# A four-layer decoder: one-head attention in staggered rounds, chosen rows for one expert layer, and smaller moves of order

## Chip, cores and metric

The kernel runs on one core of a Trainium2 chip. The metric is the device time of one execution in microseconds (us).

## What is computed

x is [8 batches, 256 tokens, 128 features] in float32, ctx has the same shape, and the mask is [8, 1, 256, 256]. Four layers follow one another. Each adds three terms to x, each computed from a layernorm of x as it then stands:

```python
x = x + L0_attn(ln(x));  x = x + L0_xattn(ln(x), ctx);  x = x + L0_ffn(ln(x))
x = x + L1_attn(ln(x));  x = x + L1_xattn(ln(x), ctx);  x = x + L1_ffn(ln(x))
x = x + L2_attn(ln(x));  x = x + L2_xattn(ln(x), ctx);  x = x + L2_ffn(ln(x))
x = x + L3_attn(ln(x));  x = x + L3_xattn(ln(x), ctx, mask);  x = x + L3_ffn(ln(x))
```

L0_attn, L0_xattn and L2_attn are softmax attention with 16 heads of 8 features, with fixed masks. L1_attn is stick-breaking attention with 16 heads. L3_xattn has 16 heads and adds the mask that is passed in. Three attentions have one head of 128 features. L1_xattn multiplies the scores by 1 + sigmoid(gate), where the gate is a second product of tanh projections. L2_xattn is causal, with projections. L3_attn has q = k = v = ln(x), and a token sees only those whose distance is a multiple of 4. L1_ffn has 8 experts of 512 hidden columns, and each expert chooses its own tokens:

```python
probs = softmax(x @ gate_w.T)                    # 256 tokens x 8 experts, per batch
g, m = top_k(probs.transpose(0, 2, 1), k=64)     # each expert takes its 64 best tokens
h = gelu(x[m] @ w1[e]) @ w2[e]
out[m] += g * h
```

L2_ffn has 16 experts (two per token, with a capacity), L3_ffn has 8 experts and a shared one.

## The kernel before

The whole of x stays in SBUF as `x_resid`, 16 tiles of 128 tokens by 128 features, two tiles per batch. The decoder (L2458) is a row of **stages**. Each is one or two blocks, in which every engine has its own instruction list, and between two blocks all engines wait for each other. A stage's name stands ahead of its buffers' names. The order is load, L0a, L0x (`quad_heads`, L435), L0n (`normalize_and_turn`, L2032), L0f (`experts`, L2163), L1a (`stick_heads`, L1340), L1x (`single_head`, L1748), L1n, L1r (`route_expert_choice`, L2292), L1f, the transfers of `load_last_experts` (L406), L2a (`quad_heads`), L2x (`single_head`), L2n, L2r, L2f, L3a (`single_head`), L3x (`masked_heads`, L936), L3n, L3r, L3s, L3f, store. The engines are PE (matmul), DVE (vector), ACT (activations, copies), POOL and SP (issues DMAs).

**`layernorm_scales`** (L117) is a block of its own ahead of each stage: ACT loads a table, then computes ln and exp of all 16 tiles' variances to get rstd. The stage's own block starts with another table load.

**`quad_heads`** treats the heads four at a time, side by side in row groups of 32. A batch has 6 slots. A slot is two score banks (`score`, L584; `hide_score`, L592, adds a fixed mask with a bf16 matmul), of which DVE takes the maxima (L864), and two banks of logits (L600) from the same products, from which the negated maximum is subtracted (`shift`), which are masked (`hide`), go through exp on ACT and are weighed with v (L645). Scores run one slot ahead of the logits. Since batch 0 has nothing to run behind, its slots come first, alone, in only two PSUM banks: DVE must reduce a bank before PE may refill it. **`masked_heads`** is alike with 8 slots. Its maxima include the mask that is loaded (L1277, four of 128x256 per slot), and PE adds the mask to the logits as three bf16 parts (L1107). Scores are one slot ahead. At the end of a batch the maxima are gathered, turned on PE (`turn_max`, L1129), negated (L1292) and only then may the next batch's logits be shifted (L1098).

**`single_head`** runs its 8 batches in a hardware loop, and the buffers (`h`, `hT`, `e`, `eT`, `y`) exist once. PE's order for a batch is scores (and gate scores L1859), turn the next h, turn exp(scores), project the next batch, weigh (L1885), and for L1x turn y (L1895), output projection. DVE takes the maximum, divides (L2005) or adds (L2013), and takes the new mean and variance of x. POOL copies the batch's ctxT into `cT`, DVE its v. In L3a the next h is made only after weighing, since h is also v.

**`normalize_and_turn`** normalizes two tiles, turns them on PE, copies them on ACT and multiplies with the router's weights, pair after pair. **`route_expert_choice`** takes the 64 best tokens of each of 64 (batch, expert) rows by eight rounds of max-8 on DVE. It leaves `gates`, zero for a token not chosen. **`experts`** for L1f runs all 2048 tokens through each of the 8 experts, batch by batch in a hardware loop. For a batch and expert PE issues 4 up matmuls of 256 columns (L2225) and 8 down matmuls of 128 columns (L2211), all recorded in halves. ACT computes two Gelu of 128x512 (L2246), DVE multiplies with the gate and adds to x (L2264).

**`load_last_experts`** is a block in which SP alone works. It issues 8 DMAs, 7.7 MB, with the weights of L2f and L3f. They may not be issued earlier, since their buffers overlap with those of earlier weights.

## Time and profile before

| what | us |
|---|---|
| device time, median of 3 runs | 2542.66 (2542.03 to 2544.7) |
| device time of the profiled execution | 2542.87 |
| its span | 2541.1 |
| PE busy in the span | 2014.9 (79%) |
| DVE busy | 1020.4 (40%) |
| ACT busy | 833.4 (33%) |
| POOL busy | 374.1 (15%) |

A stage is found in the timeline by the names of its buffers. For a stretch, the profile gives each engine's busy time, the number of instructions and PEclk, the granted share of TensorE's full clock (0.50 is 1.2 GHz, 1.00 is 2.4 GHz). The same instruction has a longer duration at the lower clock. A row of the timeline can hold several like instructions, merged, and a matmul can be recorded in two halves.

### The profile page before, as it was taken

Reading aid. Unit: us, or ns where it says so; the run is one execution under the profiler, and the core shown is the slowest. Engines: PE = TensorE matmul, PEld = TensorE weight load, DVE = VectorE, ACT = ScalarE, POOL = GpSimd, SP = SyncE. Lnnn points to the kernel's source line nnn. Section 1 sums busy time; section 2 is a strip of 40 time slices with the busy share of each in tenths; the row PEclk is TensorE's granted clock in tenths of the full one; section 3 lists DMA queues with packets and bytes.
Section 4 is the critical chain, followed back from the end, with each engine's and each line's share of the span. In section 5 each row is a group of like instructions: output and inputs, shape, how many; then the busy total and the mean of one; then the engine's idle time right before and its main releaser. Section 6 shows DMA issues by size and latency. Waiting matters only on the chain. (4 is left out here: it accounts for less than half of the span.)

```text
span 2541.1 us, 39338 instructions
## 1 busy us (share of the span) xinstructions
PE 2014.9 (79%) x13413; PEld 1346.0 (53%) x13413; DVE 1020.4 (40%) x2899; ACT 833.4 (33%) x1606; POOL 374.1 (15%) x458
## 2 busy tenths in 40 slices
PE   3898688669999564899759975499975599984998
PEld 2344244354444343799724444399953255553887
DVE  3454355334555232222125623333333355523444
ACT  2244144315777222233203432233321133332221
POOL 4331433002110000000034400000000533300000
PEclk8799599887999665899959988599975598995999
DMA  4000000000000000000120000000000000000000
GB/s 138 1 2 1 1 1 1 1 0 1 1 1 1 0 0 0 1 0 0 46 76 2 1 1 0 1 0 0 0 0 0 13 9 10 6 1 0 0 0 17
DMA packets 20029, 21.15 MB, mean 8 GB/s; under 512 B 2660, under 2 KB 15176, under 8 KB 19912
## 3 DMA queue, kind: packets, MB, share of 16 engines
q1 hardware_dynamic: 19912, 19.59, 2.4%
q8 instruction: 73, 1.20, 0.2%
q14 instruction: 44, 0.36, 0.0%
HBM read 18.54 MB, written 1.05 MB: 8 GB/s over the span
## 5 line engine op out<-in xcount | busy, mean ns | idle before, releaser
L1277 DVE CUSTOM_DVE_ANT_0 L3x_junk<-L3x_psS,L3x_mask_rows 128x256 f32<-128x256 f32 x256 | 98.6, 422 | 124.6 <-PE L3x_psS L1081 106.5
L1240 ACT ACTIVATE scores_L_experts_L<-L3x_psL 128x512 f32<-128x512 f32 x128 | 76.4, 597 | 199.4 <-PE L3x_psL L1107 196.1
L2211 PEld LDWEIGHTS L2f_psY<-scores_L_experts_L,L2f_hidden 128*128 128x128 f32 x1024 | 134.1, 193 | 8.9 <-issue 2.6
L2225 PE MATMUL L2f_psG<-hT,scores_L_experts_L 128*128 x512 | 132.5, 384 | 6.5 <-DVEq L86 6.5
L2211 PE MATMUL L2f_psY<-scores_L_experts_L,L2f_hidden 128*128 128x128 f32 x1024 | 136.0, 277 | 0.0
L2264 DVE SCALAR_TENSOR_TENSOR x_resid<-L2f_psY,L2f_gate,x_resid 128x128 f32 x256 | 78.1, 347 | 133.5 <-PE L2f_psY L2211 131.4
L2246 ACT ACTIVATE L2f_hidden<-L2f_psG 128x512 f32<-128x512 f32 x128 | 76.4, 597 | 152.4 <-PE L2f_psG L2225 152.4
L2246 ACT ACTIVATE L1f_hidden<-L1f_psG 128x512 f32<-128x512 f32 x128 | 76.4, 597 | 148.8 <-PE L1f_psG L2225 148.8
L2225 PE MATMUL L1f_psG<-hT,experts_L_L 128*128 x512 | 123.4, 385 | 2.2 <-ACTq L43 2.2
L2211 PEld LDWEIGHTS L1f_psY<-experts_L_L,L1f_hidden 128*128 128x128 f32 x1024 | 123.1, 192 | 2.9
L2211 PE MATMUL L1f_psY<-experts_L_L,L1f_hidden 128*128 128x128 f32 x1024 | 123.4, 275 | 0.0
L2264 DVE SCALAR_TENSOR_TENSOR x_resid<-L1f_psY,L1f_gate,x_resid 128x128 f32 x128 | 39.0, 347 | 170.9 <-PE L1f_psY L2211 170.9
L1107 PE MATMUL L3x_psL<-identb,L3x_mask_parts 128*128 128x256 bf16 x768 | 103.5, 289 | 0.0
L2225 PEld LDWEIGHTS L1f_psG<-hT,experts_L_L 128*128 128x128 f32 x512 | 93.5, 193 | 15.7 <-issue 5.3
L2225 PEld LDWEIGHTS L2f_psG<-hT,scores_L_experts_L 128*128 128x128 f32 x512 | 89.4, 194 | 14.6 <-issue 7.2
L1081 PE MATMUL L3x_psS<-L3x_km,L3x_qT 32*128 32x512 f32 x256 | 84.2, 738 | 13.6 <-DVE L3x_mx L1277 13.2
L2246 ACT ACTIVATE L3f_activated<-L3f_psG 128x512 f32<-128x512 f32 x72 | 43.0, 597 | 152.7 <-PE L3f_psU L2225 152.7
L804 ACT ACTIVATE L0x_probs<-L0x_psL 128x512 f32<-128x512 f32 x96 | 52.1, 595 | 121.2 <-PE L0x_psL L628 86.7
L2279 DVE TENSOR_TENSOR L3f_hidden<-L3f_activated,L3f_psU 128x512 f32<-128x512 f32 x72 | 49.5, 688 | 103.1 <-ACT L3f_activated L2246 103.1
L1089 PE MATMUL L3x_psL<-L3x_qm,ctx_T 32*128 32x512 f32 x256 | 75.7, 666 | 17.4 <-DVE L3x_mx L1277 17.0
L804 ACT ACTIVATE L2a_probs<-L2a_psL 128x512 f32<-128x512 f32 x96 | 52.1, 595 | 114.1 <-PE L2a_psL L626 84.3
L1107 PEld LDWEIGHTS L3x_psL<-identb,L3x_mask_parts 128*128 128x128 bf16 x768 | 73.5, 103 | 25.5 <-issue 14.7
(657 smaller groups left out, 4321.4 us busy)
## 6 DMA issues: line engine op xcount, KB each, us to landing
...
```

The lines of the kernel that those rows point to most:

```text
L804: nc.scalar.activation(probs[:, half, a, k, :], psL[i % RING][:], ACT.Exp, scale=scale).then_inc(s_prob, 1)
L1081: nc.tensor.matmul(psS[a][:], qT[rows, b % 3, t * P:(t + 1) * P], km[rows, b % 2, 2 * pair:2 * pair + 2, :], start=True, stop=True).then_i ...
L1089: nc.tensor.matmul(bank[:], mem.ctxT[rows, b * S + u * P:b * S + (u + 1) * P], qm[rows, b % 3, 2 * pair:2 * pair + 2, :], start=True, stop ...
L1107: last = nc.tensor.matmul(at[:, :, t * P:(t + 1) * P], parts[:, b % 2, i, t, u * P:(u + 1) * P], two, start=False, stop=i == PARTS - 1, sk ...
L1240: nc.scalar.activation(probs[:, half, a, k, :], psL[i % RING][:], ACT.Exp).then_inc(s_prob, 1)
L1277: last = nc.vector.tensor_tensor_reduce(out=junk[:, i, :], in0=psS[a][:, i * S:(i + 1) * S], in1=mrow[:, b % 2, t, :], scale=1.0, scalar=L ...
L2211: last = nc.tensor.matmul(psY[j % 2][:, t * D:(t + 1) * D], hid[:, j % 2, c, t * P:(t + 1) * P], members[j][3][:, c, :], start=c == 0, sto ...
L2225: last = nc.tensor.matmul(bank[u % 2][:, i * S:(i + 1) * S], weight[:, c * P:(c + 1) * P], source[:, bass.ds(b * S, S)], start=True, stop= ...
L2246: nc.scalar.activation(dst, psG[u % 2][:, 0:n * S].rearrange("p (c s) -> p c s", c=n), func).then_inc(s_act.sem, 1)
L2264: last = nc.vector.scalar_tensor_tensor(at, psY[j % 2][:, t * D:(t + 1) * D].unsqueeze(1), gate[:, t, members[j][4]:members[j][4] + 1], at ...
L2279: nc.vector.tensor_tensor(hid[:, j % 2, g[0]:g[0] + n, :], act_out[:, u % 2, 0:n, :], psU[u % 2][:, 0:n * S].rearrange("p (c s) -> p c s", ...
```

## The change

- The ln and exp of `layernorm_scales` move into the ACT list of the stage's own block, for all attention stages and for L1n, L2n, L3n.
- `quad_heads` (L0a, L0x, L2a): batch 0's scores come in 3 rounds of four banks (`first_scores`) in place of 6 slots of two, and later slots issue `hide_score` directly behind `score`, ahead of `shift` and `hide`.
- `load_last_experts` goes. SP issues the same 8 DMAs inside L2a's block.
- `masked_heads` (L3x): 4 opening rounds of four banks; scores run two slots ahead of the logits; the maxima and their negation have two buffers each; gathering, turning and negating the maxima come earlier, ahead of the last slots' shift.
- `lone_head` replaces `single_head`: no hardware loop, rounds in which the engines work on batches i+2 to i-2, two to four buffers of each tile, ctx and ctxT read in place. For L1x the gate's 0.5 and 1.5 are folded into one instruction and POOL adds the output bias to x. L3a's mask is one matmul of 256 columns in place of two of 128.
- `turn_and_route` replaces `normalize_and_turn` for L1n, L2n, L3n: four chunks of four tiles, each chunk with a PSUM bank of its own.
- `choose_by_expert` replaces `route_expert_choice`: besides choosing, it gives each chosen token its rank (1 to 64), by six small f32 matmuls. `chosen_experts` replaces `experts` for L1f. It makes 0/1 matrices from the ranks (DVE, two of 128x512 per batch), gathers the chosen 64 rows per expert and batch with two matmuls of 512 columns per batch, and runs 512 rows per expert instead of 2048: 32 steps of one up matmul of 512 columns, a Gelu and `widen`, and 16 down matmuls of 128 columns per expert. `widen` spreads a pair of batches' ranks and gates over 64 rows each with four matmuls of 256 columns, ACT copies the gates and DVE makes the scatter matrix (`keep_put`). Last, `scatter` adds up, per pair of batches, 8 experts in 32 matmuls of 64 rows by 128 columns.

```diff
+def last_experts(w, dram):
...
-    with nc.Block() as block:
-        @block.sync
-        def _(sp):
-            for dst, src in loads:
-                sp.dma_start(dst, src).then_inc(w["late"], 16)
-    w["late_count"] += 16 * len(loads)
...
-        layernorm_scales(nc, mem, name, scales)
...
+        w["late_count"] += 16 * len(loads)
         with nc.Block() as block:
+            if loads:
+                @block.sync
+                def _(sp):
+                    for dst, src in loads:
+                        sp.dma_start(dst, src).then_inc(w["late"], 16)
...
+                def first_scores(k):
+                    if k == 0:
+                        pe.wait_ge(s_km, 1)
+                    else:
+                        pe.wait_ge(s_red, 4 * k)
+                    t, u = KINDS[k]
+                    hidden = mask.scores[k]
+                    for r in range(4):
+                        rows = slice(32 * r, 32 * r + 32)
+                        last = nc.tensor.matmul(first_banks[r][:], qT[rows, 0, t * P:(t + 1) * P], km[rows, 0, :, u * P:(u + 1) * P],
...
+                    if b == 1:
+                        first_scores(0)
...
-                for m in range(SLOTS + 1):
-                    free_score_banks(m)
-                    for a in range(2):
-                        score(m, a)
-                    for a in range(2):
-                        hide_score(m, a)
-                    if m == SLOTS - 1:
-                        turn_max(0)
+                for k in range(1, 3):
+                    first_scores(k)
+                free_score_banks(SLOTS)
+                for a in range(2):
+                    score(SLOTS, a)
+                for a in range(2):
+                    hide_score(SLOTS, a)
+                turn_max(0)
                 for b in range(B):
...
+                            for a in range(2):
+                                hide_score(m, a)
...
-                        if ahead:
-                            for a in range(2):
-                                hide_score(m, a)
...
+                nc.scalar.activation(mem.lnv[:], mem.mv[:, :, 1], ACT.Ln, bias=mem.eps[:]).then_inc(scales, 1)
+                act.wait_ge(scales, 1)
+                nc.scalar.activation(mem.rstd[:], mem.lnv[:], ACT.Exp, scale=-0.5).then_inc(scales, 1)
...
-    SCORE_AT = ((0, 0), (2, 0), (2, 1), (2, 2), (2, 3), (0, 1), (0, 2), (0, 3))
+    SCORE_AT = ((0, 0), (0, 1), (2, 0), (2, 1), (2, 2), (2, 3), (0, 2), (0, 3))
...
+                for k in range(4):
+                    first_scores(k)
+                turn_max(0)
...
-                        m = SLOTS * (b + 1) + n + 1
+                        m = SLOTS * (b + 1) + n + 2
...
+                        if n == 6 and b > 0:
+                            project(b - 1)
+                        if n == 7 and b + 1 < B:
+                            turn_max(b + 1)
...
-                        if n == 6 and b > 0:
-                            project(b - 1)
-                        if n == 7 and b + 1 < B:
-                            turn_max(b + 1)
...
-                        if n == 7:
-                            if b + 1 < B:
-                                negate(b + 1)
...
-def single_head(nc, mem, w, name, kind):
...
+def lone_head(nc, mem, w, name, kind):
...
+    HB, TB = 4, 3
...
+                            last = nc.tensor.matmul(bank[:, t * S:(t + 1) * S], mem.identb[:], w["same"][:].unsqueeze(1).to_broadcast([P, TPB, P]),
...
+                for i in range(B + 2):
+                    if i < B:
+                        score(i)
+                    if gnosis and 0 <= i - 2:
+                        turn_y(i - 2)
+                    if not dilated and i + 1 < B:
+                        project(i + 1)
+                    if 0 <= i - 1 < B:
+                        turn_exp(i - 1)
+                    if gnosis and 0 <= i - 2:
+                        finish(i - 2)
+                    if i + 2 < B:
+                        turn(i + 2)
+                    if 0 <= i - 1 < B:
+                        weigh(i - 1)
 
...
+                for i in range(B + 2):
+                    if gnosis and i < B:
+                        gate(i)
+                    if gnosis and 0 <= i - 2:
+                        keep_y(i - 2)
+                    if not dilated and i + 1 < B:
+                        keep_projections(i + 1)
+                    if 0 <= i - 1 < B:
+                        keep_exp(i - 1)
+                    if i + 2 < B:
+                        keep_h(i + 2)
+                    if i < B:
+                        exponent(i)
...
+                        nc.vector.scalar_tensor_tensor(mixed[:, b % 2, :, :], sig[:, b % 2, :, :], 3.0,
+                                                       psS[b % 2][:].rearrange("p (t k) -> p t k", t=TPB), ALU.add, ALU.mult).then_inc(s_mixed, 1)
...
+                for i in range(B + 2):
+                    if i + 2 < B:
+                        normal(i + 2)
+                    if i < B:
+                        maximum(i)
+                    if causal and i + 1 < B:
+                        keep_v(i + 1)
+                    if 0 <= i - 1 < B:
+                        invert(i - 1)
+                    if gnosis:
+                        if 0 <= i - 2:
+                            add(i - 2)
+                        if 0 <= i - 1 < B:
+                            divide(i - 1)
+                        if 0 <= i - 2:
+                            stats(i - 2)
+                    elif 0 <= i - 1 < B:
+                        add(i - 1)
+                        stats(i - 1)
...
+def turn_and_route(nc, mem, w, name, gate, n, logits, hT=None, h_all=None):
...
+                turn(0)
+                for c in range(CHUNKS):
+                    if c + 1 < CHUNKS:
+                        turn(c + 1)
+                    pe.wait_ge(s_hT, c + 1)
+                    for t in range(c * CHUNK, (c + 1) * CHUNK):
+                        last = nc.tensor.matmul(psR[:, t * n:(t + 1) * n], hT[:, t * P:(t + 1) * P], gate, start=True, stop=True)
+                    last.then_inc(s_routed, 1)
...
+def choose_by_expert(nc, mem, w, name, logits, place, place_rows, gate_rows, E, keep):
...
+                pe.wait_ge(s_marked, 1)
+                nc.tensor.matmul(psK[:, 0:R], w["earlier"][:], marked[:, 0, :], start=True, stop=True)
+                nc.tensor.matmul(psK[:, R:2 * R], w["ones"][:], marked[:, 0, :], start=True, stop=False)
+                nc.tensor.matmul(psK[:, R:2 * R], w["earlier"][:], marked[:, 1, :], start=False, stop=True)
+                nc.tensor.matmul(psK[0:R, S:S + P], marked[:, 0, :], w["earlier"][:], start=True, stop=True)
+                nc.tensor.matmul(psK[0:R, S + P:2 * S], marked[:, 0, :], w["ones"][:], start=True, stop=False)
+                nc.tensor.matmul(psK[0:R, S + P:2 * S], marked[:, 1, :], w["earlier"][:], start=False, stop=True).then_inc(s_ranked, 1)
...
+def chosen_experts(nc, mem, w, name, h_all, place, place_rows, gate_rows, w1, w2, spread_at, E, keep):
...
+                def keep_put(i):
+                    c, e = divmod(i, E)
+                    dve.wait_ge(s_gate, i + 1)
+                    nc.vector.scalar_tensor_tensor(put[:, c, e, :], psB[i % 2][:, 0:S], w["slot_col"][:, 0:1], wide[:, i % 2, :],
+                                                   ALU.is_equal, ALU.mult).then_inc(s_put, 1)
...
+                def widen(i):
+                    c, e = divmod(i, E)
+                    if i >= 2:
+                        pe.wait_ge(s_put, i - 1)
+                    r = 2 * c * E + e
+                    for part, rows_of, one in ((0, place_rows, mem.identb), (1, gate_rows, mem.ident)):
+                        for k in range(2):
+                            last = nc.tensor.matmul(psB[i % 2][keep * k:keep * k + keep, part * S:part * S + S],
+                                                    one[0:R, r + E * k:r + E * k + 1].to_broadcast([R, keep]), rows_of[:],
+                                                    start=True, stop=True, skip_group_check=True)
+                    last.then_inc(s_wide, 1)
...
+                def scatter(c):
+                    pe.wait_ge(s_put, (c + 1) * E)
+                    if c >= 1:
+                        pe.wait_ge(s_x, 2 * c)
+                    for t in range(TPB):
+                        for e in range(E):
+                            for i in range(2):
+                                rows = slice(keep * i, keep * i + keep)
+                                last = nc.tensor.matmul(psX[i][:, t * P:(t + 1) * P], put[rows, c, e, t * P:(t + 1) * P],
+                                                        inner[rows, e, c * P:(c + 1) * P], start=e == 0, stop=e == E - 1)
+                                if t == TPB - 1 and e == E - 1:
+                                    last.then_inc(s_out, 1)
...
+                for e in range(E):
+                    for c in range(CHUNKS):
+                        up(e, c)
+                        widen(e * CHUNKS + c)
+                    if e > 0:
+                        down(e - 1)
+                down(E - 1)
+                pe.wait_ge(s_y, E)
+                for c in range(PAIRS):
+                    scatter(c)
+
...
+        lone_head(nc, mem, w, "L1x", "gnosis")
...
+            turn_and_route(nc, mem, w, "L1n", w["L1_ffn_gate_w"][:], 8, logits, h_all=h_all)
+            choose_by_expert(nc, mem, w, "L1r", logits, place, place_rows, gate_rows, 8, keep)
+            chosen_experts(nc, mem, w, "L1f", h_all, place, place_rows, gate_rows, w["L1_ffn_w1"], w["L1_ffn_w2"],
+                           w["scores"][:, 0:(B // 2) * 8 * S], 8, keep)
...
+                   wk_rot=w["L2_attn_Wk_rot"][:], wv=w["L2_attn_Wv"][:], wo=w["L2_attn_Wo"][:], mask=causal, scale=qk, loads=last_experts(w, dram))
...
```

## Rows read from the trace of the kernel before

**Rows 1.** Windows, one for each changed stage, columns as headed
```profile
core 0: us, PE busy (x) PEld busy (x) DVE busy (x) ACT busy (x) POOL busy (x), PEclk, DMA share, GB/s
42.00:256.00 214.00, 178.41 (x1496) 86.69 (x1496) 96.44 (x208) 79.13 (x150) 66.73 (x77) 0.87 0.00 1
838.50:985.50 147.00, 92.00 (x288) 58.47 (x288) 42.70 (x128) 34.82 (x85) 3.35 (x8) 0.59 0.00 0
985.50:1014.50 29.00, 10.85 (x48) 9.96 (x48) 8.20 (x24) 7.97 (x19) 0.00 (x0) 0.50 0.00 0
1028.00:1261.00 233.00, 228.60 (x1536) 212.25 (x1536) 49.41 (x176) 77.70 (x129) 0.00 (x0) 0.99 0.00 0
1261.00:1281.00 20.00, 0.00 (x0) 0.00 (x0) 0.00 (x0) 0.11 (x1) 0.00 (x0) 0.50 0.98 349
1504.00:1594.90 90.90, 46.86 (x200) 36.66 (x200) 31.13 (x112) 22.82 (x77) 3.27 (x8) 0.76 0.00 0
1875.20:1974.00 98.80, 50.98 (x176) 35.16 (x176) 30.13 (x112) 18.91 (x52) 0.00 (x0) 0.50 0.00 0
1974.00:2287.00 313.00, 264.22 (x2166) 142.77 (x2166) 143.98 (x616) 96.86 (x166) 103.84 (x116) 0.86 0.03 8
```

**Rows 2.** Timeline of L2a's opening (start us, duration, work [idle before, releaser])
```profile
1280.89 1.28 ACT L122 ACT_TABLE_LOAD   x1 [26.13 <-PEq L418]
1283.01 2.66 POOL L492 MEMSET L2a_v<- 128x3072 f32 x1 [331.95 <-SPq L489]
```

**Rows 3.** Timeline of L0a's score opening, and its PE waits (total, times, longest)
```profile
61.24 2.08 PE L584 MATMUL L0a_psS<-L0a_km,L0a_qT 32*128 32x512 f32 x4
63.89 1.29 DVE L864 TENSOR_REDUCE L0a_mx<-L0a_psS 128x4 f32<-128x512 f32 x2 [1.50 <-PE L0a_psS L592]
...
84.11 0.18 DVE L868 TENSOR_TENSOR L0a_mx<-L0a_mx_part 128x16 f32<-128x16 f32 x1
...
PE L0a_psL L600 <- DVE L0a_mx L864: 9.7, 8, 1.5
```

**Rows 4.** Timeline of L1x, tanh, product and division of one batch
```profile
882.79 0.78 ACT L1930 ACTIVATE L1x_tanh<-L1x_psG,b_gate,w_gate 128x512 f32<-128x512 f32 x1 [5.10 <-PE L1x_psG L1859]
884.17 0.69 DVE L1985 SCALAR_TENSOR_TENSOR L1x_mixed<-L1x_psS,L1x_tanh 128x512 f32<-128x512 f32 x1
892.58 0.42 DVE L2005 TENSOR_TENSOR L1x_y<-L1x_psO,L1x_rec 128x256 f32<-128x256 f32 x1 [5.40 <-PE L1x_psO L1885]
```

**Rows 5.** Timeline of L3a, a batch's weighing and its addition to x
```profile
1898.65 2.05 PE L1885 MATMUL L3a_psO<-L3a_h,L3a_eT 128*128 128x128 f32 x8 [0.77 <-ACT L3a_eT L1952]
1901.94 0.60 DVE L2013 SCALAR_TENSOR_TENSOR x_resid<-L3a_psO,L3a_rec,x_resid 128x128 f32 x2
```

**Rows 6.** Timeline of L1r, turning the chosen rows back
```profile
1026.42 0.47 PE L2354 MATMUL L1r_psC<-ident,L1r_chosen 64*128 64x64 f32 x2 [8.77 <-DVE L1r_chosen L2335]
```

**Rows 7.** Timeline of L1f: down, up, Gelu; and of L2a's last weighing
```profile
1034.44 1.95 PE L2211 MATMUL L1f_psY<-experts_L_L,L1f_hidden 128*128 128x128 f32 x16
1036.23 1.89 PE L2225 MATMUL L1f_psG<-hT,experts_L_L 128*128 x8
1037.37 0.60 ACT L2246 ACTIVATE L1f_hidden<-L1f_psG 128x512 f32<-128x512 f32 x1 [2.13 <-PE L1f_psG L2225]
...
1487.86 0.64 PE L645 MATMUL L2a_psO<-L2a_probs,L2a_v 128*32 128x256 f32 x8
```

**Rows 8.** Timeline of L3x: an opening slot; logits, scores and shift between batches
```profile
1986.52 2.08 PE L1081 MATMUL L3x_psS<-L3x_km,L3x_qT 32*128 32x512 f32 x4 [1.91 <-DVE L3x_mx L1277]
2116.86 0.70 PE L1089 MATMUL L3x_psL<-L3x_qm,ctx_T 32*128 32x512 f32 x2 [1.98 <-DVE L3x_mx L1277]
2118.83 0.61 PE L1098 MATMUL L3x_psL<-L3x_neg_max,quad_sel 32*128 32x256 bf16 x4 [0.82 <-DVE L3x_neg_max L1292]
```

**Rows 9.** The page: queue of instruction fetches (packets, MB, share); L3x's maxima on DVE
```profile
q8 instruction: 73, 1.20, 0.2%
...
L1277 DVE CUSTOM_DVE_ANT_0 L3x_junk<-L3x_psS,L3x_mask_rows 128x256 f32<-128x256 f32 x256 | 98.6, 422 | 124.6 <-PE L3x_psS L1081 106.5
```

742 lines of the change are left out of this document (487 added, 255 removed).

## The prediction, made before the run

> **What bounds the kernel now.** I read the windows by stage first [rows 1]. No engine bounds the program as a whole; each stage has its own limit, and the reader should see three kinds. In L1f PE is busy 228.6 of 233 us at a granted clock of 0.99, so only less work on PE shortens it. In L0a and L3x PE is busy 178.4 of 214 and 264.2 of 313, so waits in the opening and between batches are what an order can save. In the one-head layers nothing is full: L1x has PE 92 of 147 us, DVE 43, ACT 35, at a clock of 0.59; L3a has PE 51 of 98.8 at 0.50 (1.2 GHz). There the chain of one batch sets the time, and PE, waiting in between, is not given its full clock. L1n has PE 10.9 of 29, and for 20 us ahead of L2a only the DMA works (0.98 busy).
>
> The sum is made against the profiled run, 2542.87 us, of which 1.8 lie outside the span. It is 0.2 above the median. About 0.2%, or 5 us, is what a measurement of this kernel can tell from no change.
>
> **Scales in the stage's block.** The separate block's table load starts 2.12 us before the stage's own, and the stage's POOL work starts with the latter [rows 2]. In L0a, L0x, L2a, L1a and L3x that much goes: -2.1 each. For the other stages it is inside their sums.
>
> **quad_heads (L0a, L0x, L2a).** In the opening a slot's two scores take 2.08, then DVE's two maxima 1.29, and PE waits for them; from the first score at 61.24 to the gathering of the maxima at 84.11 the six slots take 22.9, 3.8 each [rows 3]. With four banks, four scores lie in four row groups and I take the same 2.1 for them; DVE then has four maxima, 4 x 0.65 = 2.6, of which the first starts half a us after its mask. A round is 5.1 to 5.7, and part of the first lies beside values(1): three rounds cost 17.4, so -5.5. `hide_score` ahead of `shift` lets DVE start its maxima about a us sooner in each slot; PE's waits for them ahead of the logits are 9.7 us in all in L0a [rows 3]. Not all of a wait can go, since DVE stays the slower of the two in the slots next to a batch's end: I take -4 between 0 and -10. Together -11.6 a stage, -34.8 for three, and -2.1 for L1a.
>
> **lone_head.** With staggered batches a round costs what its fullest engine needs. PE's work at full clock is busy time times PEclk [rows 1]: L1x 92.0 x 0.59 / 8 = 6.8 a batch, L2x 46.9 x 0.76 / 8 = 4.5, L3a 51.0 x 0.50 / 8 = 3.2. DVE's work a batch is 5.3, 3.9 and 3.8, ACT's 4.4, 2.9 and 2.4.
> L1x today takes about 17 a batch (147 less some 10 at its ends, by 8), in which ACT waits 5.1 for the gate scores and DVE 5.4 for weighing [rows 4]. The bias matmuls and one DVE pass leave; so a round is PE's 6.4: 8 x 6.4 = 51, plus 8 to the first scores, 4 for rounds at the low clock, 8 for the two rounds that drain, 1.3 for the barrier: 73, against 147: -74. POOL now adds the bias, 8 short additions beside 6.4 us rounds, free unless PE's `finish` waited for them, which DVE's `add` alone does.
> L2x: 8 x 4.45 = 35.6, start 9.5 (h, turn, projections, scores, one after another), low clock 3, drain 6.5, barrier 1.3, 1 for waits: 57, against 90.9: -34.
> L3a keeps a chain across rounds on DVE: weighing, then adding to x (0.60 [rows 5]), stats, the next h in two passes of 128x256 (0.42 each, as the division [rows 4]), which PE turns before it weighs again. Weighing takes 2.05 at 1.2 GHz [rows 5], 1.0 at full clock, and the round comes to 4.3: 8 x 4.3 = 34.4, start 9, low clock 3, drain 5, barrier 1.3: 53, against 98.8: -46.
> What is late next in all three is PE itself; each round is priced at the full clock. L1x's rounds keep PE busy nearly without a gap, as L1f does today. L3a's are busy 3.2 of 4.3, the least sure.
>
> **turn_and_route.** PE's 10.9 us at 1.2 GHz [rows 1] stay; with four banks only the first chunk's normalization (with rstd, 2.5) and the last copy and barrier (1.2) lie outside it: 14.5 of 29, so -14.5 in L1n and L2n and -15 in L3n: -44. The full clock would take up to 5 more off each.
>
> **choose_by_expert.** Behind the choosing come six f32 matmuls of 64 to 128 columns at the low clock. Two transposes of 64 columns are 0.47 [rows 6], so six are about 2, then a copy and two short DVE steps, part of them beside PE: +3 (between +2 and +5).
>
> **chosen_experts (L1f).** At full clock 8 down matmuls of 128 columns go by in 1.79 from start to start, 4 up matmuls of 256 in about 1.75 [rows 7]; so 0.22 a down matmul and 0.87 for 512 columns. Now per stage: 2.0 to the first 0/1 matrices; gather 8 x 2 x 0.87 = 14, with waits for DVE's matrices (two of 128x512 a batch, 0.7 each as the product in [rows 4]) and the clock's start 17.5; 0.8 for the last copy; 32 up matmuls, and 32 `widen`, each of two f32 and two bf16 matmuls of 256 columns, 2 x 0.43 + 2 x 0.11 = 1.1 one after another, 0.55 if the two column halves lie side by side. The nearest row is L2a's weighing, four f32 matmuls of 256 columns in four column groups in 0.64 [rows 7], where one after another they would be 1.73: side by side plus 0.2. So 0.85 for `widen` with its entry, 1.05 for `up` with its own, 32 x 1.9 = 61. Down: 128 x 0.22 with a drain each time, 8 x 4.1 = 33. ACT has a Gelu (0.60) and a copy (0.4) per step, DVE 0.45: both within 1.9. Scatter: 32 matmuls of 0.22 are 7.0 one after another, half of it side by side; I take 5.6, plus 2.1 in which PE waits for DVE's addition: 4 x 7.7 = 31. With 1 ahead of it and 1.5 at the end: 148, against 233: -85. Bounds: 128 if nothing is paid for going from one shape to the other and halves run together, 171 if all halves run one after another and the scatter waits more.
> The Trainium skill, "TensorEngine Tiling (Array Packing)", Tiling Modes, Key Properties, says that tiles of one shape run in parallel and that changing the shape drains the array. That rule speaks against alternating `up` and `widen`. The trace agrees as far as the side-by-side weighing goes; what the drain costs no row shows alone, and by the rule two changes a step at the 0.2 above would be 13 of the 61, which is already in it.
>
> **Transfers in L2a.** The 20 us alone go [rows 1]. Their cover is L2a, 210 us long, which itself loads nothing; L2f needs them 300 us later. What they can delay is instruction fetch and SBUF access in L2a's opening: 0 to +20. I take 0: the transfers write buffers that no engine touches in L2a, and no row shows one stage slowed by another's DMA.
>
> **L3x.** -2.1 for the scales. The opening's eight slots of 4.0 (2.08 of scores behind a wait of 1.91 [rows 8]) become four rounds of 2.1 + 8 maxima of 0.422 [rows 9] + 0.3 = 5.75, 23 in all, and one slot more comes ahead of the loop: -4 to -5. Between batches PE waits 1.98 for the maxima ahead of the logits and 0.82 ahead of the shift [rows 8]; with scores two slots ahead and the maxima turned earlier most of these 2.8 go at 7 boundaries: -19. DVE gains no work (144 of 313 busy). -25, between -5 and -33.
>
> **Sum.** -34.8 - 2.1 - 74 - 44 + 3 - 85 - 20 - 34 - 46 - 25 = -362. 2542.9 - 362 = 2181.
>
> **The rivals.**
> (a) PE is not given its full clock in the one-head rounds. For it: all three are at 0.50 to 0.76 now, L3a at 0.50 throughout. Then a round is PE's work at 1.2 GHz: L1x 12.8 less what the first rounds had anyway, +37; L2x +25; L3a 6.4, +13: 2256. Chance 9%. In L3a alone: 2194, in the main case's range.
> (b) The halves of `widen` and scatter run one after another: +23, 2204. For it: no row shows f32 halves of 64 columns. Against it: four groups of 32 do run together. 17%.
> (c) The transfers, or fetching the longer unrolled code, hold up L2a's opening and the new stages: +20, 2201. 12%.
> (d) The ends of the stages are better than taken, L1f at 128 and L2n, L3n at a higher clock: 2150. 17%.
> (e) The hidden cover isn't there in L3x and quad_heads, DVE being the one that sets their slots: the 19 and 3 x 4 stay, 2212. 8%.
> (f) Slower: the instruction stream. Loops become straight code, so some 60 more fetches of 16 KB are needed than today's 73 [rows 9]. If each held all engines up by more than 362 / 60 = 6 us, the gain would be gone, 2550. Against it: 73 fetches leave PE 79% busy today, and L0a's straight code, 178 of 214 busy, shows no such holes. 1.5%.
> That the change does not do what it says, no overlap in the rounds because a wait ties batch i to i-1, would leave the one-head layers as they are: 2335, 2%.
>
> **How the numbers follow.** The main case has 33%, at 2181 with 2165 to 2197 as its own range. With (b), (c), (d), (e) and half of (a), 2130 to 2250 holds about 8 in 10. Faster by over 0.2% is every case but (f): 0.98; within 0.2% 0.005; slower 0.015.
>
> **What the profile after would show.** L1x, L2x and L3a in windows of about 73, 57 and 53 us with PEclk above 0.85; if it is near 0.5, (a). L1f of 148 with a step of 1.9 between Gelus; 2.5 means (b). Nothing between L1f's and L2a's barrier, and the queue q1 busy inside L2a; gaps on all engines there mean (c). No wait of 1.98 ahead of L3x's logits between batches. L1n, L2n and L3n of 14 to 15. The prediction is wrong if the rounds are set by chains between engines longer than PE's work, which adds 8 us per us of round in each one-head stage.

## The result, and the profile after

The changed kernel takes 2120.09 us (median of 4 runs, 2119.14 to 2122.51), the kernel before 2543.68 beside it: a ratio of 0.8336, with a 95% interval of 0.8322 to 0.8351. The forecast was 2181 with a range from 2130 to 2250. The direction and the places were right, but 61 us more went than forecast. The profiled run's span is 2120.8 us.

I measure a stage from the last named instruction of the stage ahead to its own last one, so that the barrier counts, and set it beside the sum's terms. L0a alone is taken from its first instruction to L0x's, since the loading ahead of it moves by 3 us from run to run. The barrier between L0a and L0x, 2.1 us shorter, so stands in both rows, and the column adds up to 424.5 where the two profiled spans differ by 420.3; the loading took 1.4 us more in the changed kernel's, and the rest is spread over stages that the change leaves alone.

| stage | before | after | measured | forecast |
|---|---|---|---|---|
| L0a | 214.0 | 206.0 | -7.9 | -11.6 |
| L0x | 231.5 | 217.8 | -13.8 | -11.6 |
| L1a | 277.0 | 274.4 | -2.6 | -2.1 |
| L1x | 146.0 | 58.9 | -87.1 | -74 |
| L1n, L2n, L3n together | 96.5 | 46.6 | -49.9 | -44 |
| L1r | 13.0 | 16.8 | +3.7 | +3 |
| L1f | 231.1 | 124.2 | -106.8 | -85 |
| transfers and L2a | 243.7 | 214.7 | -29.0 | -31.6 |
| L2x | 90.0 | 47.7 | -42.3 | -34 |
| L3a | 98.8 | 39.7 | -59.1 | -46 |
| L3x | 314.0 | 284.3 | -29.7 | -25 |

The windows of the changed kernel that answer to [rows 1], here L1x, L2x and L3a from their first to their last named instruction, then L1f, L3x and L1n:

```profile
core 0: us, PE busy (x) PEld busy (x) DVE busy (x) ACT busy (x) POOL busy (x), PEclk, DMA share, GB/s
818.31:875.15 56.84, 50.13 (x258) 33.87 (x258) 30.96 (x92) 33.14 (x85) 6.15 (x8) 0.92 0.00 1
1250.13:1294.01 43.88, 35.11 (x200) 28.22 (x200) 26.11 (x100) 19.30 (x73) 0.00 (x0) 0.88 0.00 1
1562.70:1597.63 34.93, 25.61 (x160) 19.96 (x160) 24.95 (x92) 16.65 (x49) 0.00 (x0) 0.93 0.01 1
908.00:1033.00 125.00, 114.48 (x800) 68.06 (x800) 34.20 (x88) 41.72 (x81) 0.00 (x0) 0.98 0.00 1
1599.50:1884.00 284.50, 246.00 (x2166) 135.43 (x2166) 131.96 (x609) 95.67 (x166) 104.04 (x116) 0.92 0.03 9
877.50:892.00 14.50, 10.35 (x48) 9.86 (x48) 5.73 (x11) 3.73 (x8) 0.00 (x0) 0.53 0.01 2
```

The three one-head layers now have PEclk at 0.88 to 0.93. L1f lost half of its matmul records and is still bound by PE, busy 114.5 of 125.0 us. The timeline of PE in L1x and L3a of the changed kernel:

```profile
824.85 2.08 PE L1907 MATMUL L1x_psS<-ctx_T,L1x_hT 128*128 128x256 f32 x4
...
852.39 1.03 PE L1907 MATMUL L1x_psS<-ctx_T,L1x_hT 128*128 128x256 f32 x4
857.24 1.16 PE L1945 MATMUL L1x_psO<-ctx_nat,L1x_eT 128*128 128x128 f32 x8
858.24 1.03 PE L1907 MATMUL L1x_psS<-ctx_T,L1x_hT 128*128 128x256 f32 x4
...
1579.70 0.60 PE L1907 MATMUL L3a_psS<-L3a_hT 128*128 128x256 f32 x2
1582.36 0.44 PE L1874 MATMUL L3a_psT<-ident,L3a_h 128*128 128x128 f32 x2 [0.97 <-DVE L3a_h L2085]
1582.63 1.06 PE L1945 MATMUL L3a_psO<-L3a_h,L3a_eT 128*128 128x128 f32 x8
1583.53 0.60 PE L1907 MATMUL L3a_psS<-L3a_hT 128*128 128x256 f32 x2
```

The first scores of L1x, at 824.85, take 2.08 us: 1.2 GHz. Those at 852.39 take 1.03. A round of L1x is 858.24 - 852.39 = 5.85 us, of which PE waits only 0.14 (for `eT`, ahead of weighing). A round of L2x is 4.30, with a wait of 0.43 for ACT's copy of `eT`. A round of L3a is 3.83, and PE waits 0.97 in it for the next h on DVE: that is the chain of the forecast.

### The profile page after: what moved, and what is told of

Its sections match the earlier page's. It is cut to its first block and busy times, and to the rows that moved or that the text cites. A ratio compares the mean times of both kernels' runs of the same rounds, so it can differ in the third digit from the quotient of the medians.

```text
span 2120.8 us, 35006 instructions
## 1 busy us (share of the span) xinstructions
PE 1796.1 (85%) x12643; PEld 1123.5 (53%) x12643; DVE 966.9 (46%) x2700; ACT 773.7 (36%) x1518; POOL 375.8 (18%) x451
## 3 DMA queue, kind: packets, MB, share of 16 engines
HBM read 18.54 MB, written 1.05 MB: 9 GB/s over the span
## 5 line engine op out<-in xcount | busy, mean ns | idle before, releaser
L2418 DVE SCALAR_TENSOR_TENSOR x_resid<-L2f_psY,L2f_gate,x_resid 128x128 f32 x256 | 78.0, 346 | 133.3 <-PE L2f_psY L2365 131.1
L2400 ACT ACTIVATE L2f_hidden<-L2f_psG 128x512 f32<-128x512 f32 x128 | 76.5, 597 | 152.1 <-PE L2f_psG L2379 152.1
L1324 DVE CUSTOM_DVE_ANT_0 L3x_junk<-L3x_psS,L3x_mask_rows 128x256 f32<-128x256 f32 x224 | 86.3, 422 | 91.8 <-PE L3x_psS L1112 83.7
L1150 PE MATMUL L3x_psL<-identb,L3x_mask_parts 128*128 128x256 bf16 x768 | 95.9, 275 | 0.0
L830 ACT ACTIVATE L2a_probs<-L2a_psL 128x512 f32<-128x512 f32 x96 | 52.1, 594 | 108.6 <-PE L2a_psL L648 73.8
L830 ACT ACTIVATE L0a_probs<-L0a_psL 128x512 f32<-128x512 f32 x96 | 52.1, 594 | 104.6 <-PE L0a_psL L648 68.8
L2365 PE MATMUL L3f_psY<-experts_L_L,L3f_hidden 128*128 128x128 f32 x576 | 77.1, 277 | 4.9 <-DVE L3f_hidden L2433 4.9
L2365 PEld LDWEIGHTS L3f_psY<-experts_L_L,L3f_hidden 128*128 128x128 f32 x576 | 74.3, 191 | 10.9 <-issue 8.0
L2379 PE MATMUL L3f_psG<-hsT,experts_L_L 128*128 x256 | 66.9, 384 | 2.1 <-DVEq L43 2.1
L1557 PE MATMUL L1a_psL<-L1a_soft_near,neg_tri 128*128 128x512 f32 x128 | 67.8, 611 | 0.0
L1112 PE MATMUL L3x_psS<-L3x_km,L3x_qT 32*128 32x512 f32 x224 | 66.0, 666 | 1.9 <-DVE L3x_mx L1324 1.9
```

Of the source, the lines that this page charges most:

```text
L830: nc.scalar.activation(probs[:, half, a, k, :], psL[i % RING][:], ACT.Exp, scale=scale).then_inc(s_prob, 1)
L1112: nc.tensor.matmul(psS[a][:], qT[rows, b % 3, t * P:(t + 1) * P], km[rows, b % 2, 2 * pair:2 * pair + 2, :], start=True, stop=True).then_i ...
L1150: last = nc.tensor.matmul(at[:, :, t * P:(t + 1) * P], parts[:, b % 2, i, t, u * P:(u + 1) * P], two, start=False, stop=i == PARTS - 1, sk ...
L1324: last = nc.vector.tensor_tensor_reduce(out=junk[:, i, :], in0=psS[a][:, i * S:(i + 1) * S], in1=mrow[:, b % 2, t, :], scale=1.0, scalar=L ...
L1557: last = nc.tensor.matmul(bank(s, a)[:], w["neg_tri"][:], soft(s, a), start=False, stop=kk == 0, skip_group_check=True)
L2365: last = nc.tensor.matmul(psY[j % 2][:, t * D:(t + 1) * D], hid[:, j % 2, c, t * P:(t + 1) * P], members[j][3][:, c, :], start=c == 0, sto ...
```

## The experiments

All but the first edit the changed kernel, so their times stand against 2120. The kernel before ran beside them at 2541.6 to 2543.8. A ratio is to that kernel, with its interval. A stage that an edit does not touch can still come out differently: L2x took 42.5 to 44.7 us in the runs that left it as it is, with PEclk between 0.90 and 0.84. So a small edit is judged by the length of its own stage, and the total stands beside it.

**One part alone.** The kernel before with `lone_head` only, in its three places:

```diff
-        single_head(nc, mem, w, "L1x", "gnosis")
+        lone_head(nc, mem, w, "L1x", "gnosis")
```

> The kernel before with one part of the change: lone_head in place of single_head in L1x, L2x and L3a, all else as before. Theory A (the parts add up): the changed kernel lost 87.1, 42.3 and 59.1 us from the end of the stage ahead to the end of these three, so 188.5, and 2543 - 188 = 2355. Theory B (straight code costs fetches, or the other parts were needed beside it): the stages come out longer than 56.8, 43.9 and 34.9 us, and the kernel above 2362.

Measured: 2349.95, ratio 0.9244 (0.9226 to 0.9263), with 57.0, 43.6 and 35.7 us for the three stages. Theory A: the part brings 192 us by itself where 188 to 189 were expected, and the straight code costs nothing that shows. The three stages themselves gave 188.0; most of the rest lies in L3x, which the edit left alone and which came out 3.8 us shorter behind the new L3a.

**Order against loop.** The three lists of `lone_head` in the old order; for PE:

```diff
-                for i in range(B + 2):
-                    if i < B:
-                        score(i)
...
+                for i in range(B):
+                    score(i)
+                    if not dilated and i + 1 < B:
+                        turn(i + 1)
+                    turn_exp(i)
+                    if not dilated and i + 1 < B:
+                        project(i + 1)
+                    weigh(i)
+                    if dilated and i + 1 < B:
+                        turn(i + 1)
+                    if gnosis:
+                        turn_y(i)
+                        finish(i)
```

> The changed kernel with one edit: lone_head's three lists are put in the order of the kernel before, one batch after another, still without a hardware loop and with all its buffers. In the kernel before the first to the last named instruction took 141.3 us in L1x, 85.4 in L2x, 93.4 in L3a; in the changed one 56.8, 43.9, 34.9. Theory A (the staggered order carries the gain): 130 to 138, 80 to 84, 88 to 92, so 2290 to 2300. Theory B (the loop with its counting and the missing buffers carried a good part): each stage at least 15 us below its length before, so under 2265.

Measured: 2256.35, ratio 0.8875 (0.8855 to 0.8894). In L1x, L2x and L3a:

```profile
815.25:928.90 113.65, 73.69 (x258) 47.48 (x258) 31.68 (x92) 34.88 (x85) 5.82 (x8) 0.68 0.00 1
1304.99:1378.54 73.55, 50.60 (x200) 40.76 (x200) 26.54 (x100) 20.99 (x73) 0.00 (x0) 0.66 0.00 0
1646.13:1731.62 85.49, 50.62 (x160) 32.85 (x160) 25.77 (x92) 17.11 (x49) 0.00 (x0) 0.52 0.00 0
```

Neither theory holds in full. The order carries 137 us of the three stages' 184 (57 + 30 + 51). The rest, 28 in L1x, 12 in L2x and 8 in L3a, comes without it, from what the code also drops: the loop with its counting, buffers that exist once, the copies of ctx, L1x's bias matmuls and one pass of DVE. Which of these brings how much I did not separate.

**The clock's share.** The same, and in L3a PE is kept busy where it would wait:

```diff
+                def fill(n):
+                    if dilated:
+                        for _ in range(n):
+                            nc.tensor.matmul(psQ[:], mem.identb[:], w["same"][:].unsqueeze(1).to_broadcast([P, 4, P]), start=True, stop=True)
```

> The same as e8_batch_by_batch, and in L3a alone PE computes bf16 products nobody reads (16 of 128x512 a batch) where it would wait, so that it is busy. Theory A (half of PE's time in L3a was its low clock): PEclk near 1.00 in L3a, PE's useful 51 us take 26, and L3a is 22 to 28 us shorter than in e8, so the order itself is worth the remaining 30. Theory B: the clock stays at 0.50 or the fillers cost what they bring: L3a as long as in e8 or longer.

```profile
1651.12:1716.98 65.86, 55.85 (x280) 31.38 (x280) 25.77 (x92) 17.08 (x49) 0.00 (x0) 0.94 0.00 1
```

Measured: 2238.93 (0.8789 to 0.8818). L3a fell from 85.5 to 65.9 us with 120 more records on PE, and PEclk rose from 0.52 to 0.94. So of the 50.6 us that the order saves in L3a, at least 19.6 are to be had by the clock alone (the added products may themselves hold up useful work), and up to 31 need the order. Its size is a little below theory A's 22. The kernel as a whole gained 17.4 by the medians and 12.3 between the profiled runs, where L1x and L3x, which differ in nothing, came out 3.8 and 2.0 longer. L1x and L2x were not tried with such products, so the clock's share in them is not shown.

**The mask matmuls of quad_heads.** First back to their old place, then between `shift` and `hide`:

```diff
-                            for a in range(2):
-                                hide_score(m, a)
                         if n == 0:
                             pe.wait_ge(s_nm, b + 1)
                         shift(b, n)
+                        if ahead:
+                            for a in range(2):
+                                hide_score(m, a)
                         for a in range(2):
                             hide(b, n, a)
```

> The changed kernel with one edit: in quad_heads the hide_score matmuls stand behind shift and hide again, as in the kernel before; the four-bank opening stays. In the changed kernel a batch takes 21.19 us in L0a, 22.89 in L0x, 21.81 in L2a; before it took 20.37, 22.71, 20.99. Theory A: the move put a full-array matmul between two row-group ones, so every masked slot pays about 0.2 us for two more changes of shape; then the batches fall back to 20.4, 22.7 and 21.0, and the kernel is 11 to 13 us faster than the 2120 of the changed one. Theory B: the batches are longer for another reason (transfers, the opening's banks) and hide_score ahead saves DVE's waits as forecast; then this kernel is 4 to 12 us slower than 2120.

> The changed kernel with one edit: in quad_heads the order is score, shift, hide_score, hide, so that DVE can start about 0.3 us sooner than with hide_score last, with no more changes of shape than before. Theory A (shape changes cost 0.2 a masked slot): batches of 20.4, 22.7 and 21.0 us or up to 0.3 less, 2108 or a little less. Theory B (an early hide_score costs because it delays the logits and so ACT's exp): about half of the loss stays, L0a near 20.8.

The first gave 2117.15 (0.8306 to 0.8343), the second 2102.97 (0.8258 to 0.8285). A batch takes, in us:

| | L0a | L0x | L2a |
|---|---|---|---|
| before | 20.37 | 22.71 | 20.99 |
| changed | 21.19 | 22.89 | 21.81 |
| mask matmuls last | 20.36 | 22.71 | 20.99 |
| mask matmuls between | 20.35 | 21.82 | 20.98 |

The first slot of a batch of L0a in the changed kernel, and with the mask matmuls between:

```profile
145.34 0.59 PE L588 MATMUL L0a_psS<-L0a_km,L0a_qT 32*128 32x512 f32 x2
145.87 0.60 PE L596 MATMUL L0a_psS<-causal,identb 128*128 128x512 bf16 x2
146.41 0.39 PE L636 MATMUL L0a_psL<-L0a_neg_max,quad_sel 32*128 32x256 bf16 x4
146.73 0.39 PE L648 MATMUL L0a_psL<-identb,causal 128*128 128x256 bf16 x2
```

```profile
119.84 0.59 PE L588 MATMUL L0a_psS<-L0a_km,L0a_qT 32*128 32x512 f32 x2
120.31 0.39 PE L636 MATMUL L0a_psL<-L0a_neg_max,quad_sel 32*128 32x256 bf16 x4
120.64 0.60 PE L596 MATMUL L0a_psS<-causal,identb 128*128 128x512 bf16 x2
121.08 0.38 PE L648 MATMUL L0a_psL<-identb,causal 128*128 128x256 bf16 x2
```

The shape goes 32, 128, 32, 128 rows in the first and 32, then 128 in the second: two changes more. From slot to slot the changed kernel needs 0.16, 0.20, 0.23 and 0.23 us more than the one before in L0a's four masked slots, and the same in the two without a mask, 0.82 a batch: theory A, 0.1 us a change. A change of number type does not explain it, since both orders change between f32 and bf16 equally often. Back in the old place the total gained only 3 us of theory A's 11 to 13, less than its four runs differ among themselves (2112.8 to 2121.0); the three stages together were 4.2 us shorter. The gain is so small since the first and the last batch, where PE waits for DVE's maxima, did profit from the early mask matmuls (L0x's first batch grew from 22.4 to 24.0). Between, both gains come together. L0x, masked in all six slots, shows both sides at once: 0.18 longer in the changed kernel, 0.89 shorter than before with the mask matmuls between.

**Changes of shape in L1f.**

```diff
-                    for c in range(CHUNKS):
+                    for c in range(0, CHUNKS, 2):
                         up(e, c)
+                        up(e, c + 1)
                         widen(e * CHUNKS + c)
+                        widen(e * CHUNKS + c + 1)
```

> The changed kernel with one edit: in L1f two up matmuls are followed by two widen groups, so that the array changes its shape half as often. A step is 1.71 us in the changed kernel. Theory A (a change of shape costs about 0.1 us, as the moved mask matmuls of L0a showed with 0.2 a pair): 32 changes fewer, -3.2 us in L1f, step 1.61. Theory B (no price between full-array and 64-column shapes): 0, or a small loss where PE then waits for a free bank.

Measured: 2116.70 (0.8311 to 0.8338). L1f went from 123.3 to 118.3 us and an expert from 10.43 to 9.80, with 4 changes of shape instead of 8: 0.16 us each. Theory A, with a higher price than forecast. The number type changes as often as before (each `widen` is two bf16 and then two f32 matmuls), so it does not carry the price. The total fell by 3.4 us only, since L2a and L2x came out 1.8 longer. One `widen` in the middle of a pair:

```profile
935.15 0.59 PE L2674 MATMUL L1f_psB<-gate_rows,ident 64*64 64x256 f32 x4
935.58 0.27 PE L2674 MATMUL L1f_psB<-place_rows,identb 64*64 64x256 bf16 x2
```

Its two f32 matmuls of 256 columns, one for each half and recorded in two parts each, take 0.43 us from their start to that of the next work. That is what a single one of 256 columns takes at full clock: the parts of L1x's score matmuls follow each other every 0.216 us, two parts to a matmul. So the halves run side by side.

**Halves one after another.**

```diff
                     for t in range(TPB):
-                        for e in range(E):
-                            for i in range(2):
+                        for i in range(2):
+                            for e in range(E):
```

and in `widen` likewise.

> The changed kernel with one edit: in L1f, widen and scatter issue all matmuls of one half (64 columns or 64 rows) before those of the other, so that no two neighbours lie in different halves. In the changed kernel a step of up and widen is 1.71 us and a scatter's 32 matmuls 3.84. Theory A: neighbours in different halves run side by side, which is why L1f came out shorter than forecast; then a step becomes 2.1 to 2.2, a scatter about 7, and the kernel is 14 + 13 = 27 us slower, 2147. Theory B: half-size matmuls are merely quick by themselves: no change, 2120.

Measured: 2127.67 (0.8351 to 0.8379). The changed kernel's first three scatters with the waits ahead of them, then the first of this experiment, then one of its `widen`:

```profile
1010.11 3.84 PE L2703 MATMUL L1f_psX<-L1f_inner,scores_L_experts_L 64*128 64x128 f32 x64 [0.68 <-ACT L1f_inner L2729]
1014.88 3.84 PE L2703 MATMUL L1f_psX<-L1f_inner,scores_L_experts_L 64*128 64x128 f32 x64 [0.93 <-DVE x_resid L2633]
1020.50 3.84 PE L2703 MATMUL L1f_psX<-L1f_inner,scores_L_experts_L 64*128 64x128 f32 x64 [1.78 <-DVE x_resid L2633]
```

```profile
1009.16 6.39 PE L2703 MATMUL L1f_psX<-L1f_inner,scores_L_experts_L 64*128 64x128 f32 x64 [0.68 <-ACT L1f_inner L2729]
```

```profile
932.52 0.30 PE L2674 MATMUL L1f_psB<-place_rows,identb 64*64 64x256 bf16 x2
932.66 0.60 PE L2674 MATMUL L1f_psB<-gate_rows,ident 64*64 64x256 f32 x4
```

The scatter agrees with theory A: 6.39 against 3.84, so neighbours in different row halves run side by side. The two halves also write different PSUM banks, which this run does not separate from the halves; `widen`, whose halves share a bank, runs side by side too (above). That is 10 us for four scatters, of which 3 come back as shorter waits for DVE. The step of `up` and `widen` is 1.72 against 1.71. There each half has only one bf16 and one f32 matmul, and the second half's still run beside the first half's: the last two rows show both bf16 matmuls done within 0.30 us, and the f32 ones after them, though the order of issue is bf16, f32, bf16, f32.

**Four banks for scatter.**

```diff
+        outs = psX + psU
...
-                    if c >= 1:
-                        pe.wait_ge(s_x, 2 * c)
+                    if c >= 2:
+                        pe.wait_ge(s_x, 2 * (c - 1))
...
-                                last = nc.tensor.matmul(psX[i][:, t * P:(t + 1) * P], put
+                                last = nc.tensor.matmul(outs[2 * (c % 2) + i][:, t * P:(t + 1) * P], put
```

> The changed kernel with one edit: scatter takes turns over four PSUM banks instead of two, so that PE need not wait for DVE's addition of the pair just done. In the changed kernel PE waits 0.93, 1.78 and 1.77 us there. Theory A: those waits go, -4 us, 2116. Theory B: DVE's additions and stats (about 3.4 us a pair against 3.84 of PE) take over as the limit: -1 or less.

Measured: 2113.33 (0.8299 to 0.8327); L1f 118.1 us, 5.2 less, and L2x, not touched, 1.4 less. Theory A: the scatters follow each other every 3.6 us without a wait.

**The transfers.**

```diff
+        loads = last_experts(w, dram)
+        with nc.Block() as block:
+            @block.sync
+            def _(sp):
+                for dst, src in loads:
+                    sp.dma_start(dst, src).then_inc(w["late"], 16)
```

> The changed kernel with one edit: the 8 weight transfers stand in a block of their own ahead of L2a again. Theory A (they are hidden in L2a and slow nothing there): 20 us slower, L2a's own length unchanged at 212.3 us. Theory B (inside L2a they delay its opening): the loss is smaller than 20, and L2a alone becomes shorter by the difference.

Measured: 2140.93 (0.8405 to 0.8433), L2a itself 212.9 us against 212.3. Theory A: they are hidden and slow nothing.

**L3x.** First `project` and `turn_max` issued behind `hide` and `weigh` again, and nothing else:

```diff
-                        if n == 6 and b > 0:
-                            project(b - 1)
-                        if n == 7 and b + 1 < B:
-                            turn_max(b + 1)
                         shift(b, n)
...
                             weigh(b, 1)
+                        if n == 6 and b > 0:
+                            project(b - 1)
+                        if n == 7 and b + 1 < B:
+                            turn_max(b + 1)
```

> The changed kernel with one edit: in masked_heads PE issues project and turn_max behind hide and weighing again, as before; scores stay two slots ahead. A batch of L3x is 29.88 us in the changed kernel, 33.8 before. Theory A (the two slots of lead alone took the wait away): a batch stays below 30.2. Theory B (turning the maxima early is what frees the next batch's shift): a batch goes back by 1.5 to 3 us, the kernel to 2130 to 2140.

Measured: 2141.05 (0.8403 to 0.8436). L3x grew from 282.4 to 302.8 us, its batches from 29.88 to between 32.4 and 34.0. PE's waits in L3x (line it waits at, releaser: us in total, times, longest), changed kernel and experiment:

```profile
PE L3x_psL L1132 <- DVE L3x_mx L1324: 11.3, 16, 2.0
```

```profile
PE L3x_psL L1132 <- DVE L3x_mx L1324: 21.7, 16, 2.8
```

That looked like theory B, and stronger. But DVE's list still had `negate` ahead of the slot's maxima, so DVE stood waiting for a turning that PE now issued late (10.9 us in 7 waits, the longest 3.2, where it had been 7.8 and 1.7), and gave the score banks back late. PE's added waits are only half of the 20 us; the clock is the other half, as the windows below show. So I put both lists in the old order:

```diff
-                        if n == 6 and b + 1 < B:
-                            gather_max(b + 1)
                         if n == 7 and b + 1 < B:
-                            negate(b + 1)
+                            gather_max(b + 1)
                         if m < SLOTS * B:
                             reduce(m)
...
+                        if n == 7:
+                            if b + 1 < B:
+                                negate(b + 1)
```

> The changed kernel with masked_heads in the old order on both engines: PE issues project and turn_max behind hide and weighing, DVE gathers at the last slot and negates behind that slot's maxima. Scores stay two slots ahead, with the two buffers for the maxima. A batch is 29.88 us in the changed kernel, 32.4 to 34.0 with only PE's order put back, 33.8 before. Theory A (the lead alone takes the waits away; PE's late turning only clashed with DVE's early negating): 29.9 to 31, L3x at 283 to 291. Theory B (the next batch's shift is late whenever the maxima are turned late): 32.4 or more, L3x at 300 or more.

Measured: 2117.29 (0.8322 to 0.8350), L3x at 279.5 us, 2.9 below the changed kernel, its batches at 29.88 again. One steady batch of the kernel before, the changed kernel, PE's order alone put back, and both orders put back:

```profile
2116.86:2150.72 33.86, 30.80 (x271) 17.26 (x271) 18.51 (x78) 11.63 (x20) 12.67 (x15) 0.90 0.04 9
1727.45:1757.33 29.88, 28.52 (x270) 16.22 (x271) 16.29 (x77) 11.63 (x20) 12.66 (x15) 1.00 0.03 10
1733.44:1767.44 34.00, 30.94 (x270) 17.45 (x271) 17.30 (x77) 11.63 (x20) 12.74 (x15) 0.90 0.03 9
1722.76:1752.64 29.88, 27.94 (x271) 16.49 (x271) 17.57 (x77) 11.64 (x20) 12.77 (x15) 1.00 0.04 11
```

Theory A: the lead is enough, and the earlier turning earns nothing. The lead stands here for scores two slots ahead, two buffers for the maxima, and a negation that is one pass of DVE shorter; these were not separated. It does not take all waits away. At a steady batch's boundary PE waited 1.98 and 0.83 before, waits 1.06 in the changed kernel, 2.8 with PE's order alone put back, and 0.91 and 0.77 with both. But the same matmuls keep PE busy 28.5 us at a PEclk of 1.00 in the changed kernel, and 30.8 at 0.90 in the one before: with the longer waits the clock dropped at each boundary (0.50 from 2118 to 2124 us), with the shorter ones it held. The reading of the first run was wrong; what it shows is that two lists in different orders cost 20 us, 10.4 of them in PE's waits and 10.3 in its busy time (256.3 against 246.0 us).

**A busy PE ahead of the routing.** Seven bf16 products of 128x512 that nobody reads, at the start of L1n, L2n, L3n:

```diff
+                for _ in range(7):
+                    nc.tensor.matmul(psF[:], mem.identb[:], w["same"][:].unsqueeze(1).to_broadcast([P, 4, P]), start=True, stop=True)
                 turn(0)
```

> The changed kernel with one addition: in L1n, L2n and L3n PE starts with 7 bf16 products of 128x512 that nobody reads, in the time in which it waits for the first h (about 3 us). Theory A (PE's clock there is low because PE stood idle ahead): PEclk rises within the stage and each of the three is 2 to 5 us shorter, 2106 to 2114. Theory B (the stage is over before the clock rises, or the filler delays the first transposes): PEclk stays at 0.50 and each stage is 0 to 1 us longer.

Measured: 2117.18 (0.8302 to 0.8337). From the stage ahead to the routing behind it is 3.1 us less in L3n (PEclk 0.66), 0.8 less in L1n (0.69) and nothing in L2n (0.50). Theory A in size for L3n alone. In L1n the added products followed each other every 0.22 us, the full clock that L1x had left; behind them PE stood idle for 0.9 and 0.7 us between short pieces of work, and from 5 us after the first product its matmuls took the time of the low clock.

**Three edits together.** Mask matmuls between, scatter over four banks, and four `widen` together over four banks:

```diff
-                    for c in range(CHUNKS):
-                        up(e, c)
-                        widen(e * CHUNKS + c)
+                    up(e, 0)
+                    up(e, 1)
+                    for c in range(CHUNKS):
+                        widen(e * CHUNKS + c)
+                    up(e, 2)
+                    up(e, 3)
```

> The changed kernel with three edits together: hide_score between shift and hide; in L1f four widen groups stand together between two pairs of up matmuls (2 changes of shape a group of four steps instead of 8), with four banks for widen; scatter over four banks. Alone the first gave 2103, two by two 2116.7 (5.0 us in L1f), four banks 2113.3 (5.2 in L1f), against 2120. Theory A (every change of shape costs 0.15 us in L1f): 8 x 6 x 0.15 = 7 us from widen, so 2120 - 17 - 7 - 5 = 2091. Theory B (it was not the changes but a wait that the pairs removed): 2094 or more, and L1f no shorter than 113 us.

Measured: 2090.05 (2089.56 to 2090.97, 5 runs), ratio 0.8219 (0.8206 to 0.8233), with L1f at 110.6 us. That is the sum of the three parts, and 30 us below the changed kernel. An expert takes 9.48 us, 0.32 less than two by two for two changes of shape fewer: 0.16 each again.

**The same with a busy PE.** In L1n and L3n nine idle products ahead and two behind the second chunk.

> The kernel of e10_all_three with idle products on PE at the start of L1n and L3n (9) and behind the second chunk (2), where 7 at the start had brought 0.8 and 3.1 us. Theory A (the clock falls in L1n for want of work between the chunks): PEclk above 0.8 in both, 3 to 4 us each, 2083. Theory B (the fillers stand in the way of the transposes as much as they quicken them): 2086 to 2088.

Measured: 2083.64 (2082.41 to 2084.10), ratio 0.8200 (0.8186 to 0.8213). PEclk is 0.83 in L1n and 0.78 in L3n, and they are 3.5 and 2.6 us shorter than in the changed kernel. Theory A for the total and for L1n. L3n stays below its 0.8 and 3 us, and with more products it gained less than with seven (3.1), at a higher PEclk: there they begin to stand in the way, as theory B said. This is the fastest kernel run, 36 us below the changed one. L3x's old order, which was 2.9 us faster by itself, was not put into it.

## Why the prediction was wrong

**Direction and places: right.** Each part moved its own stage, no stage grew but L1r, and the next limit in L1x and L2x is PE at full clock, in L3a the chain by way of DVE. Rivals (a), (c) and (f) did not come: PEclk is 0.88 to 0.93, the transfers cost nothing, and `lone_head` alone on the kernel before kept its gain. Of (e) the half on L3x did not come; the half on quad_heads did, and went further, for another reason than it gave (below). The page now has 82 instruction fetches against 73 [rows 9], not 60 more: that estimate was far off.

**The one-head layers, 34 of the missing 60 us.** Most of it is the stages' ends. The forecast put 8 whole rounds, then a start, a drain and 3 to 4 us of low clock on top: 21 us in L1x and L2x, 18 in L3a. Measured, a stage less 8 rounds is 58.9 - 46.8 = 12.1, 47.7 - 34.4 = 13.3 and 39.7 - 30.6 = 9.1. Two errors lie in this. The rounds that fill and drain a pipeline do part of the same 8 batches' work, so the last are short: from weighing to weighing L1x's last two rounds take 4.76 and 3.46 in place of 5.85. And the low clock costs little where PE waits anyway: in L1x it lasts for 11 us behind the stage ahead, of which PE waits 5.1 for the barrier, the first h and its copy. How the 8 to 9 us a stage divide between the two errors no run shows.

The smaller part, 9 us, is PE's work in a round, which the forecast took as busy time times PEclk, by 8: 6.8, 4.5 and 3.2. That product is no measure of work. L2x issues the same 200 matmul records in three kernels, and has 46.86 x 0.78 = 36.6 before, 50.60 x 0.66 = 33.4 batch by batch and 35.11 x 0.88 = 30.9 in the changed kernel. PEclk is a mean over the window, also over its idle time, while the busy time gathers where PE was slow; and the record of a lone matmul is longer than what it adds when others follow it: L3a's two turnings at 1582.36 last 0.44, and the weighing behind them starts after 0.27. The first row here is of the kernel before:

```profile
1506.58:1591.98 85.40, 46.86 (x200) 36.66 (x200) 30.01 (x107) 20.85 (x73) 3.27 (x8) 0.78 0.00 0
```

Counted in single records at the full clock, from the changed kernel's trace, a round of L1x is 12 parts of 256-column matmuls at 0.216, 12 parts of 128-column ones at 0.112 and 8 turnings at 0.109: 4.8 us. Of the missing 1.05, 0.6 lies where the round changes between full and 64-wide shapes (the gate scores and their projections), four times a round at 0.15 as in L1f, and 0.4 ahead of and at the start of weighing. The forecast had no term for these changes in L1x. The DVE chain of L3a was put at 4.3 and measured 3.83; which of its links were shorter was not taken apart.

**L1f, 22 us.** No term of the sum was missing, and nearly all were too large. Step by step: gather 16.1 (forecast 17.5), the step of `up` and `widen` 1.71 (1.9, so 6 in 32; `up` is 1.06 as forecast, `widen` 0.66 and not 0.85), down 3.67 an expert (4.1, so 3.5), scatter 21.5 with its waits (31). The scatter was 9.5 of the 22: the forecast took 5.6 of 7.0, "half of it side by side", where all of it is, 3.84. L2a's weighing in [rows 7], four groups in 0.64 against 1.73, had said so, and I weighed it only for `widen`. Rival (b) was the opposite of what happened, and (d), which bounded L1f at 128, was still 4 short. A price for changing shape was rightly in the sum: 13 us forecast, and 0.16 x 64 = 10 by the runs. The Trainium skill, "TensorEngine Tiling (Array Packing)", Tiling Modes, Key Properties, says that a change of tiling mode drains the array; it gives no price. The runs agree, with 0.16 us a change.

**quad_heads.** The opening was under-forecast. The maxima of batch 0 are turned 5.3 us earlier in L0a though its stage began 1.4 later, and the first batch, from that turning to the next, is 2.9 us shorter, 21.2 against 24.1: 9.6 in all where 5.5 were forecast. The forecast -4 for `hide_score` failed by its sign: a steady batch grew by 0.82 in L0a and L2a and by 0.18 in L0x, and with the shorter first and last batches the move cost 4.2 us over the three stages, where -12 was forecast. The step at fault is the one that named only what DVE gains. Two changes of shape more in each masked slot had no term; their price is 0.1 us a change by the runs. The rule of the Trainium skill, "TensorEngine Tiling (Array Packing)", Tiling Modes, Key Properties, that a change of tiling mode drains the array, was weighed for `widen` and not for this move. The runs agree with it here too: 0.82 us a batch for eight changes more.

**L3x.** -29.7 against -25: the steady batch is 29.88, where 33.8 less the 2.8 of waits would be 31. The number is close partly by luck. Of the 4.0 us a batch, PE's idle time gives 1.7 (3.06 to 1.36), not 2.8, since a wait of 1.06 stayed at the boundary; the other 2.3 are PE's busy time, 30.80 to 28.52, because the clock no longer drops there. The forecast had no term for that. It named the lead and the early turning together as the cause; with both orders put back, the lead is all of it.

**The routing stages.** They now take 15.5 each from the stage ahead, where they took 32.2. The window of L1n in [rows 1] began 3 us behind L1x's last instruction and left out the barrier and part of the separate scale block, of which about 2 a stage went too. PEclk is still 0.50 in all three. The 5 us a stage that the full clock might bring were named and not counted; products that nobody reads got 3.5 and 2.6 of them in L1n and L3n.

The rest, the transfers (-20, measured 20.8), L1a and L1r, was as forecast.

**The range.** It reached 50 us below the forecast for errors of single terms. All large terms were rounded to the careful side, 13 + 13 + 8 + 22 + 6 + 5, and such errors add up instead of cancelling. Only `hide_score` went the other way.
